# Written-out batches and a DMA swap of rotary halves in a one-core transformer kernel

## What is computed

```python
c_q    = hidden_states @ w_q_down                  # 192 wide
q_nope = (c_q @ w_q_up_nope)                       # 32 heads x 128
q_rope = _apply_rope((c_q @ w_q_up_rope), ...)     # 32 heads x 64
...
scores = (einsum(q_lat, c_kv) + einsum(q_rope, k_rope)) / sqrt(192)
probs  = softmax(where(causal, scores, min))
out    = einsum(einsum(probs, c_kv), wuv) @ w_out
...
def _apply_rope(x, ...):                           # x1, x2: first and second 32 of 64 rows
    return concatenate([x1 * c1 - x2 * s2, x1 * s2 + x2 * c2])
```

## Time and profile before

| what | before |
|---|---|
| median of 3 runs (lowest to highest) | 1193.83 us (1193.36 to 1195.86) |
| the profiled execution, own time | 1193.11 us |
| its span in the profile | 1191.3 us |
| mean granted TensorE clock | 0.991 |
| PE busy, share of the span | 1114.5 us, 94% |
| DVE, ACT, POOL busy | 908.1, 622.5, 740.8 us (76, 52, 62%) |

### The profile page before, as it was taken

One profiled execution on the slowest core, in us unless ns is written; L12 is line 12 of the kernel. 1 busy time (PEld: TensorE's weight loads), 2 busy tenths in 40 slices (PEclk: granted clock), 3 DMA queues, 4 the chain that ended last, 5 costly groups with the idle time before them and its releaser, 6 DMA issues.

```text
span 1191.3 us, 23885 instructions
## 1 busy us (share of the span) xinstructions
PE 1114.5 (94%) x7284; PEld 917.3 (77%) x7284; DVE 908.1 (76%) x2990; ACT 622.5 (52%) x1732; POOL 740.8 (62%) x951
## 2 busy tenths in 40 slices
PE   5997999999987999999998799999998899999997
PEld 4755788888786788888878578888878678888876
DVE  4767888878665888888775788887866788888855
ACT  3554655555443655555534465555544365565542
POOL 2406877777332987877621687777733398777741
PEclk9998999999999999999999999999999999999999
DMA  9550000000101000000100100000010100000000
GB/s 288 170 186 1 1 2 2 1 2 1 37 10 64 2 1 2 1 1 1 36 1 36 37 2 1 1 1 2 1 37 18 55 1 1 2 1 1 1 2 36
DMA packets 22264, 31.13 MB, mean 26 GB/s; under 512 B 9302, under 2 KB 11094, under 8 KB 21498
## 3 DMA queue, kind: packets, MB, share of 16 engines
q1 hardware_dynamic: 19770, 24.85, 6.5%
q10 hardware_dynamic: 2368, 4.72, 1.2%
HBM read 22.23 MB, written 4.19 MB: 22 GB/s over the span
## 4 chain that ended last, share of the span: by engine, by line
PE 78%; DVE 7%; issue 5%; POOL 4%; ACT 3%; SPq 1%; DMA 1%; POOLq 0%; DVEq 0%; ACTq 0%
PE Y L986 15%; PE Y L960 12%; PE XZ L945 11%; PE Y L909 10%; PE XZ L926 6%; PE XZ L925 6%; PE XZ L924 6%; PE Y L680 4%; PE XZ L655 2%; POOL prob L636 1%; PE XZ L680 1%; ACT xT_hi L1040 1%; POOL qT_lo L547 1%; POOL q_sums L542 1%; DVE q_turned L1561 1%
## 5 line engine op out<-in xcount | busy, mean ns | idle before, releaser
L1226 ACT ACTIVATE prob<-XZ,small 128x512 f32<-128x512 f32 (+3 forms) x512 | 266.7, 526 | 290.5 <-DVE small L1622 290.4
L636 POOL TENSOR_TENSOR prob<-prob,small 128x512 f32<-128x512 f32 (+3 forms) x512 | 361.2, 723 | 55.5 <-DVE small L1574 38.8
L1622 DVE CUSTOM_DVE_ANT_0 XZ<-XZ,mask 128x512 f32<-128x512 f32 (+3 forms) x512 | 245.0, 510 | 119.3 <-issue 117.0
L542 POOL TENSOR_TENSOR q_sums<-q_sums,q_turned 64x512 f32<-64x512 f32 (+2 forms) x130 | 164.4, 1264 | 196.0 <-DVE q_turned L1562 193.6
L945 PE MATMUL XZ<-ident,prob 128*128 128x128 f32 x1280 | 196.3, 276 | 4.6 <-POOL prob L636 4.2
L924 PE MATMUL XZ<-kT_hi,qT_hi 128*128 128x512 f32 (+3 forms) x512 | 177.5, 347 | 16.4 <-issue 6.5
L547 POOL TENSOR_TENSOR qT_lo<-q_sums,qT_hi 128x512 fp32r<-128x512 f32 (+2 forms) x130 | 165.3, 1271 | 37.9 <-ACT qT_hi L1193 37.1
L945 PEld LDWEIGHTS XZ<-ident,prob 128*128 128x128 f32 x1280 | 149.7, 140 | 44.8 <-issue 15.7
L925 PE MATMUL XZ<-kT_lo,qT_hi 128*128 128x512 f32 (+3 forms) x512 | 165.7, 324 | 0.0
L926 PE MATMUL XZ<-kT_hi,qT_lo 128*128 128x512 f32 (+3 forms) x512 | 165.6, 323 | 0.0
L960 PE MATMUL Y<-probT,ckv 128*64 128x384 f32 (+2 forms) x1280 | 152.3, 383 | 2.8 <-issue 0.2
(11 more groups left out here) (221 smaller groups left out, 2191.4 us busy)
## 6 DMA issues: line engine op xcount, KB each, us to landing
wout_nat<-in_L_attn_w_out_dram SPq DMA_DIRECT2D x16, 512.0 KB, 4.8
out_dram<-x_sb SPq DMA_DIRECT2D x16, 256.0 KB, 2.0
x_next<-_attn_hidden_states_dram SPq DMA_DIRECT2D x12, 256.0 KB, 3.6
x_sb<-x_next SPq DMA_DIRECT2D x12, 256.0 KB, 2.4
wbase_nat<-in_L_ffn_W_base_dram ACTq DMA_DIRECT2D x1, 1024.0 KB, 5.6
x_sb<-_attn_hidden_states_dram ACTq DMA_DIRECT2D x4, 256.0 KB, 6.8
nope_a<-_L_attn_w_q_up_nope_dram ACTq DMA_DIRECT2D x1, 1024.0 KB, 5.6
rope_a<-_L_attn_w_q_up_rope_dram SPq DMA_DIRECT2D x1, 1024.0 KB, 8.2
```

The costliest lines, as they stand in the source:

```text
L542: nc.gpsimd.tensor_tensor(q, q, turned, ALU.add).then_inc(q_sum_set, 1)
L636: last = nc.gpsimd.tensor_tensor(prob[u % RING][:, c:c + w], prob[u % RING][:, c:c + w], inv_sum[:, u % RING, m:m + 1].broadcast_to([P, w] ...
L1226: last = nc.scalar.activation(prob[u % RING][:, c:c + w], score_ps[u % 2][:, c:c + w], ACT.Exp, bias=neg_max[:, u % RING, m:m + 1], scale= ...
L1622: last = nc.vector.tensor_tensor_reduce(bank, bank, mask[:, S - w:S], -1.0, HIGHEST, ALU.add, ALU.min, neg_max[:, u % RING, m:m + 1])
```

## The change

Four edits. (1) The loops of all engines go: batches 0 to 2 are written out like batch 3, SP's loop over weight loads too, and `alone(b)` replaces the tests for a loop register. (2) In the pairs' query chain DVE makes one sine product of 64 rows into rows 0 to 63 of `q_turned` and signals it, then the cosine product; SP moves the two halves of 32 rows into rows 64 to 127, each in the other's place, with two DMAs of 64 KB per head. The queries made in `mixed_steps` and the opening stay with `q_rotary`. (3) On POOL `q_sum` goes behind the probabilities of its slot and also waits for the DMAs, and `qT_low` goes two slots behind it; on ACT `qT_high` goes behind the exponential of its slot. (4) A small DVE memset in each slot goes.

```diff
+                def swap_turns(b):
+                    for n in range(1, PAIRS):
+                        for head in range(2):
+                            sp.wait_ge(q_sin_set, swap_index(b, n, head) + 1)
+                            for j in range(2):
+                                sp.dma_start(q_turned[n % 2][64 + 32 * j:96 + 32 * j, head, :],
+                                             q_turned[n % 2][32 - 32 * j:64 - 32 * j, head, :]).then_inc(q_swapped[head], 16)
...
                 opening()
-                with loop(sp, 0, NB - 1) as b:
+                for b in range(NB - 1):
+                    swap_turns(b)
                     sequence(b)
+                swap_turns(NB - 1)
...
-                        if k < 4 and within(g, u, UNITS * LAST_PAIR - 1):
-                            m = q_index(b, BODY_PAIRS * g + p + 1, k // 2)
-                            if k % 2:
-                                qT_low(m, k // 2, (p + 1) % 2)
-                            else:
...
-                                q_sum(m, k // 2, (p + 1) % 2)
+                        n1 = BODY_PAIRS * g + p + 1
+                        queries = within(g, u, UNITS * LAST_PAIR - 1)
+                        if k in (2, 4) and queries:
+                            qT_low(q_index(b, n1, k // 2 - 1), k // 2 - 1, n1 % 2)
                         if within(g, u, SLOTS - 1):
...
                             last.then_inc(prob_scaled, 1)
+                        if k in (0, 2) and queries:
+                            pool.wait_ge(prob_scaled, 80 * b + BODY * g + u + 1)
+                            pool.wait_ge(q_swapped[k // 2], 32 * (15 * b + n1))
+                            q_sum(q_index(b, n1, k // 2), k // 2, n1 % 2)
...
+                def q_parts(m, head, par, bank):
+                    dve.wait_ge(q_done, m + 1)
+                    nc.vector.tensor_tensor(q_turned[par][0:64, head, :], bank[64:P, :], sinT[64:P, :],
+                                            ALU.mult).then_inc(q_sin_set, 1)
+                    nc.vector.tensor_tensor(q_sums[par][:, head, :], bank, cosT[:], ALU.mult).then_inc(q_rot_set, 1)
...
-                            nc.vector.memset(wait_slots[:, u % RING:u % RING + 1], 0.0)
...
-                            q_rotary(q_index(b, n1, k // 2), k // 2, (p + 1) % 2, qT_ps[k // 2])
+                            q_parts(q_index(b, n1, k // 2), k // 2, (p + 1) % 2, qT_ps[k // 2])
```

More of the change, by code:

```diff
@@ L158, in build @@
         ones, eps, minus_half = columns(52, 2), columns(54, 1), columns(55, 1)
-        wait_slots = small[0:1, 56:60]
+        warm_slot = small[0:1, 56:60]
         region_a = [cursor[0]]
@@ L268, in build @@
         FOLDS = {8: ((9,), (10,)), 9: ((11,), (12,)), 10: ((13,), (14,)), 11: ((15,), ())}
[L270 to L278, removed]
         def first(i):
@@ L308, in build @@
         turns_in, turns_one = sem("turns_in"), sem("turns_one")
+        q_sin_set, q_swapped = sem("q_sin_set"), [sem(f"q_swapped{i}") for i in range(2)]
         y_ps, y_added = sem("y_ps"), sem("y_added")
@@ L317, in build, with alone @@
         MIXED = len(ORDER)
+        def alone(b):
+            return b in (-1, NB - 1)
         def place_of(b, s):
-            return s if isinstance(b, int) else ORDER.index(s)
+            return s if alone(b) else ORDER.index(s)
         def ffn_of(b, s):
-            return s if isinstance(b, int) else (s + FIRST) % DOWN
+            return s if alone(b) else (s + FIRST) % DOWN
         def tile_of(b, s):
@@ L335, in banks_of @@
         def banks_of(b, s):
-            if not isinstance(b, int):
+            if not alone(b):
                 return ORDER_BANKS[ORDER.index(s)]
@@ L343, in x_tile @@
         def x_tile(b, s):
-            return x_next[s % ST][:] if s >= FIRST and not isinstance(b, int) else x_sb[:, s % ST, :]
+            return x_next[s % ST][:] if s >= FIRST and not alone(b) else x_sb[:, s % ST, :]
         def attention(slot_work, tail):
@@ L405, in q_index, with swap_index @@
             return 32 * b + 2 + 2 * n + head
+        def swap_index(b, n, head):
+            return 30 * b + 2 * (n - 1) + head
         SLOTS = UNITS * PAIRS
@@ L483, in opening @@
                     sp.dma_start(sin_sb[:], rope_sin).then_inc(tables_in, 16)
-                    rounds(sp, PAIRS // SLOTS_OUT, load_out)
+                    for r in range(PAIRS // SLOTS_OUT):
+                        load_out(r)
                     sp.dma_start(sinT[64:P, :], rope_sinT).then_inc(turns_in, 16)
@@ L639, in work @@
                             last.then_inc(prob_scaled, 1)
+                        if k in (0, 2) and queries:
+                            pool.wait_ge(prob_scaled, 80 * b + BODY * g + u + 1)
+                            pool.wait_ge(q_swapped[k // 2], 32 * (15 * b + n1))
+                            q_sum(q_index(b, n1, k // 2), k // 2, n1 % 2)
                     attention(work, 0)
                 opening()
-                with loop(pool, 0, NB - 1) as b:
+                for b in range(NB - 1):
                     attend(b)
@@ L1003, in last_outputs @@
                         output_products(two, oT_buffer(PAIRS - 1), t, 1, last_out_ps[t]).then_inc(y_ps, 1)
-                        if t == 1 and not isinstance(b, int):
+                        if t == 1 and not alone(b):
                             transpose_x(b, FIRST)
@@ L1029, in _ @@
                 opening()
-                with loop(pe, 0, NB - 1) as b:
+                for b in range(NB - 1):
                     attend(b)
@@ L1158, in norm @@
                     elif i < FIRST:
-                        act.wait_ge(shift_set, 2 * b + (2 if isinstance(b, int) and s else 1))
+                        act.wait_ge(shift_set, 2 * b + (2 if alone(b) and s else 1))
                     else:
@@ L1212, in work @@
                             oT_high(b, g, p)
-                        if k in (2, 4) and queries:
-                            qT_high(q_index(b, n1, k // 2 - 1), k // 2 - 1, (p + 1) % 2)
                         v = u - T_LAG
@@ L1229, in work @@
                             last.then_inc(prob_set, 1)
+                        if k in (2, 4) and queries:
+                            qT_high(q_index(b, n1, k // 2 - 1), k // 2 - 1, (p + 1) % 2)
                         if copies and k != 2:
@@ L1234, in _ @@
                 opening()
-                with loop(act, 0, NB - 1) as b:
+                for b in range(NB - 1):
                     attend(b)
@@ L1243, in row_stats @@
                 def row_stats(b, s):
-                    if s < DOWN and not isinstance(b, int) and s >= FIRST:
+                    if s < DOWN and not alone(b) and s >= FIRST:
                         dve.wait_ge(x_in[s - FIRST], 16 * (b + 2))
@@ L1642, in _ @@
                 opening()
-                with loop(dve, 0, NB - 1) as b:
+                for b in range(NB - 1):
                     attend(b, True)
```

7 lines of the change are left out of this document (1 added, 6 removed).

## The result

The change takes 1210.34 us (median of 4 runs, 1209.51 to 1213.43) against 1193.61 us before (4 runs); the ratio is 1.0141, 95% interval 1.0119 to 1.0162. It is slower by 17 us, and 1211 was forecast. The profiled execution took 1210.27 us, its span is 1208.3 us.

A forecast was written before the change was run, and what follows sets the result against it. PE's own work bounds the steady pairs now; after the change a circle of 13.8 us would. +7.9 + 5.5 + 11.7 - 5.0 - 2.3 = +17.8 us on 1193.1 gives 1211 us, range 1192 to 1226.

The forecast's parts named there:

- The circle: From PE's slot 1 (S) to the next pair's, through ACT's copy, exponential, `qT_high` and POOL's five pieces: 13.8 us.
- PE's wait: Sign: PE idle ahead of slot 1's scores for `qT_lo`, some 0.3 us in pairs 3 to 13, over 1 in pair 15.
- pair 14: Pair 14 to slot 1 of pair 15, four times: 13.8 us instead of 12.34 or 12.47, +5.5 us.
- pairs 0 to 2: First three pairs of each batch, without output products in slot 1: 12.3 us a pair, +11.7 us over four batches.
- pairs 3 to 13: Eleven steady pairs of each batch at 13.8 us, 151.8 us a batch: +7.9 us over four batches.
- starts of batches: Starts of batches 1 and 2, written out, go from 7.14 and 7.38 us to 4.77: -5.0 us.
- tail, mixed steps: Each batch's tail with the mixed steps, 78.06 us, gains 1.0% when written out, three times: -2.3 us.
- The DMAs: Two 64 KB moves of halves per head on SP's queue land in 2.4 us, hidden, at no cost.
- The first rival: Only the written-out batches count: the circle stays under PE's 13.49 us, 1177 us in all; chance 13%.
- The room of 4.7 us: Time head 0's halves have behind the sine product before `q_sum` must start to meet ACT's turn: some 4.7 us.
- Part 2: Less DVE work, one 0.69 us product per head and five memsets a pair fewer: costed at nothing.

The follow-up runs named there:

- e4: The change without its DMAs: DVE makes the two sine products of 32 rows in place, ACT's and POOL's moves stay; 1214.47 us.
- e9: The change with one idle POOL addition (0.40 us) ahead of the scaling of slot 2, inside the circle; 1234.40 us.
- e10: The change with the same idle POOL addition ahead of the scaling of slot 0, where POOL had stood idle, outside the circle; 1212.73 us.
- e1: The kernel before with its batch loops written out and nothing else; 1182.34 us.
- e5: The kernel before with batch loops written out and POOL's new order alone; ACT's order as before, no DMAs; 1242.45 us.
- e3: The change with ACT's `qT_high` back ahead of the copy and the exponential of its slot, nothing else; 1220.23 us.
- e2: The kernel before with batch loops written out and ACT's `qT_high` behind the exponential of its slot; POOL's order as before, no DMAs; 1221.95 us.
- e6: The change with its DMAs issued behind the cosine product instead of the sine product, 0.73 us later; 1221.97 us.

## Why the prediction was right

**The circle** is right, piece by piece: copy at S + 5.27 (5.24 foreseen), POOL's `qT_low` from 7.37 (7.40), end at 13.68 (13.72), PE at 13.73 (13.77). e4, e9 and e10 exclude the halves and POOL's load as its cause. PE's wait is put down to POOL's `qT_lo`, as foreseen, but as idle time it shows in pair 14 and pairs 0 to 2, hardly in the steady ones.

**The terms of the sum**, in us, by the two profiles:

| term | forecast | measured |
|---|---|---|
| pairs 3 to 13 | +7.9 | +4.8 |
| pair 14 | +5.5 | +5.1 |
| pairs 0 to 2 | +11.7 | +13.2 |
| starts of batches | -5.0 | -4.8 |
| tail, mixed steps | -2.3 | -1.1 |
| opening and end | 0 | -0.2 |
| sum | +17.8 | +17.0 |

- Pairs 3 to 13: I rounded 13.77 up to 13.8, and it is 13.73. 44 pairs make 3 us of 0.07.
- Pairs 0 to 2: 12.32 in the rule, as taken (12.3). The miss is one pair of 13.90 in batch 2, which comes from the clock (see below).
- Tail and mixed steps: 0.38 us a batch, half of the 1.0% that I gave them; why only half is not shown. The misses of -3.1 (pairs 3 to 13), +1.5 (pairs 0 to 2) and +1.2 us largely cancel: the sum is better than its terms, and that part is luck.
- Starts: PE's idle time of 3.06 us is batch 1's; at batch 2's start it reads 3.43. The term goes by the lengths of the stretches and holds.

**The pair of 13.90** is pair 1 of batch 2. Its halves were in time, but TensorE's granted clock fell in it, behind 2.45 us in which PE stood idle for `qT_lo`. PE's line, then the stretches of pair 1 of batch 1, pair 1 of batch 2, and the part of the latter behind the idle time:
```profile
681.88 0.50 PE L933 MATMUL XZ<-kT_hi,qT_hi 128*128 128x512 f32 x1 [2.45 <-POOL qT_lo L558]
```
```profile
398.12:410.44 12.32, 10.98 (x75) 8.81 (x75) 7.52 (x27) 7.44 (x22) 10.64 (x13) 1.00 0.08 18
681.88:695.78 13.90, 12.56 (x74) 10.24 (x74) 7.62 (x27) 7.43 (x22) 10.62 (x13) 0.88 0.04 10
682.44:686.17 3.73, 3.73 (x15) 3.35 (x14) 2.25 (x9) 0.78 (x2) 2.85 (x3) 0.56 0.00 0
```
The last reads 0.56, so most of it ran at the 1.2 GHz level, and the pair is 1.58 us longer than its like at full clock. The sum has no term for this: it put the clock in pairs 0 to 2 at nothing. The DMAs are not needed for it, since e4 without them has such a pair too (14.24); e10 has three, which make most of what its profiled execution took above the change's. That the idle time brings the clock down is read from this order of events; no run here varies it.

**The DMAs** cost nothing, as taken, as long as they have their room. The first rival's 1177 us was 4 to 5 us too low for its own case, as e1 shows. The room of 4.7 us was 0.35 too wide, and I gave none for head 1, whose 4.25 is the tighter.

**Part 2**, DVE's lighter list at nothing, holds in the steady pairs (e4: 151.00 against 151.04), but not in pairs 0 to 2, where e4 reads 4.4 us more than the change (3.5 of it in pair 0), nor under e5's order: e3, the same order with the DMAs and the lighter list, takes 22 us less.

**What I did not see** is how the parts hang together. The prediction treats ACT's and POOL's moves as one lump; that either alone is worse than both, and that ACT's move buys the halves their room, came from e2, e3 and e5 only.

In the change's steady pairs POOL is busy 117.31 of 151.05 us and DVE 15 us less than in e1 (109.26 against 124.54). The Trainium skill (Perfetto Trace Analysis, Identifying the Most-Contended Engine) says to optimize the engine with the highest occupancy first and takes occupancy as a fair measure for GpSimd. By that alone POOL had room. The trace doesn't agree: the 2.3 us more for eleven pairs (151.05 against 148.73) came from the order on engines that were not the busiest, POOL at 78%.

## What to carry to other kernels

Where engines hand work round in a fixed order, sum one whole round trip, from an instruction of one pass to the same one in the next, and compare it with the busiest engine's own pace; what is longer sets the time, and occupancy doesn't show it. Then look for the next circle below: here 13.73, 13.55 and 13.49 lay one under the other, so that undoing any single part gained little or lost. A transfer hidden in such a circle must be judged by its slowest landings, not by its median. And where a circle leaves PE idle, look at the granted clock behind the idle time too.

## What the runs showed of the hardware

- The 64 KB transfers within SBUF (two for each head, 120 pairs of them) land 2.56 to 2.62 us behind the product for most, yet 17 of 60 of head 0's came later than 3.2 us, up to 4.1, in stretches whose DMA engines were 9% busy.
- The same pair of transfers one behind the other's landing takes 3.9 us, not twice 2.6.
- In one pair of the change the granted clock fell behind 2.45 us in which PE stood idle: 682.44:686.17 reads 0.56, and the pair took 13.90 us. Its like at a granted clock of 1.00 took 12.32.
- The last releaser in the profile can be a bystander: 65.5 us were put down to a DMA which, taken away, left 60.2 us of the same wait; and a real wait for halves (1.80 us in e3, 0.93 in e6) was put down to DVE.
